# First attention of a four-layer block: loads and weight splits inside it, units begun half a chain apart

## What is computed

```
a = attention(n, n, n, Wq, Wk, Wv, causal) + n          # n = layer norm of x
h = layer_norm(a, gamma, beta)
c = attention(h, context, context, Wcq, Wck, Wcv) + h   # not causal
h = layer_norm(c, gamma, beta)
out = relu(layer_norm(relu(h @ W1 + b1) + h, gamma, beta))
x = x + tanh(g_xattn[0]) * out
```

## Time and profile before

| | us |
|---|---|
| median of 3 runs | 3161.24 (3153.39 to 3162.49) |
| the profiled execution | 3154.09 |
| its span, first to last instruction | 3151.9 |
| start of the first projection (QT of unit 0) | 43.01 |
| start of QT of unit 2 | 160.68 |
| first instruction of the next phase | 293.13 |

### The profile page before, as it was taken

How to read it: one execution, slowest core, us unless ns; L and a number is a source line. 1 busy time by engine, 2 the same in 40 slices (tenths; PEclk the granted TensorE clock), 3 DMA queues, 4 the chain that set the end, 5 groups by cost and what they waited for, 6 DMA issues and landing times. The chain is left out here.

```text
span 3151.9 us, 55831 instructions
## 1 busy us (share of the span) xinstructions
PE 2588.4 (82%) x18079; PEld 2360.7 (75%) x18080; DVE 1555.5 (49%) x3598; ACT 1246.0 (40%) x3047; POOL 1231.6 (39%) x1183
## 2 busy tenths in 40 slices
PE   4674468369979999938997988999689998799992
PEld 4564468269978888828997867888578988789992
DVE  3665545556634444445553324443468777343332
ACT  3232134134543333304553433444357666433330
POOL 0012361564320856041001646640445664266313
PEclk9786689589979999969997889999889999799996
DMA  3041254310010434120000634430611110033312
GB/s 116 1 134 48 72 167 137 94 34 17 16 31 11 140 105 145 33 76 21 15 15 27 222 118 119 114 95 27 191 41 41 55 41 14 28 117 118 109 48 89
DMA packets 139055, 239.80 MB, mean 76 GB/s; under 512 B 17681, under 2 KB 89645, under 8 KB 136609
## 3 DMA queue, kind: packets, MB, share of 16 engines
q1 hardware_dynamic: 65536, 134.62, 13.9%
q10 hardware_dynamic: 59424, 64.09, 6.1%
q0 software_dynamic: 13824, 37.53, 3.9%
HBM read 162.35 MB, written 73.79 MB: 75 GB/s over the span
## 5 line engine op out<-in xcount | busy, mean ns | idle before, releaser
L564 ACT ACTIVATE moe_act<-moe_gu 128x256 f32<-128x256 f32 (+1 forms) x431 | 189.2, 439 | 608.4 <-PE moe_gu L95 608.4
L323 POOL TENSOR_TENSOR moe_wlo<-moe_raw,moe_whi 128x768 fp32r<-128x768 f32 (+1 forms) x170 | 342.1, 2012 | 36.7 <-issue 12.9
L847 DVE TENSOR_TENSOR moe_h<-moe_act,moe_gu 128x256 f32<-128x256 f32 x321 | 134.8, 420 | 367.5 <-ACT moe_act L564 365.5
L352 POOL DMA_INDIRECT moe_whi<-rows_y,moe_slot_r x144 | 139.4, 968 | 423.1 <-DMA rows_y<-moe_y 380.4
L93 PE MATMUL moe_yp<-moe_whi,moe_hThi 128*128 (+1 forms) x926 | 291.2, 314 | 8.9 <-DVE moe_hTlo L863 8.6
L93 PE MATMUL moe_gu<-moe_whi,moe_xThi 128*128 (+2 forms) x706 | 280.4, 397 | 0.1
L95 PE MATMUL moe_gu<-moe_whi,moe_xTlo 128*128 (+2 forms) x706 | 264.3, 374 | 0.0
L94 PE MATMUL moe_gu<-moe_wlo,moe_xThi 128*128 (+2 forms) x706 | 263.9, 374 | 0.0
L94 PE MATMUL moe_yp<-moe_wlo,moe_hThi 128*128 (+1 forms) x926 | 261.0, 282 | 0.0
L95 PE MATMUL moe_yp<-moe_whi,moe_hTlo 128*128 (+1 forms) x926 | 260.4, 281 | 0.0
L863 DVE TENSOR_TENSOR moe_hTlo<-moe_tp,moe_hThi 128x256 fp32r<-128x256 f32 (+1 forms) x275 | 145.1, 528 | 232.1 <-ACT moe_hThi L570 231.1
(11 more groups left out here) (484 smaller groups left out, 7920.8 us busy)
## 6 DMA issues: line engine op xcount, KB each, us to landing
moe_raw<-in_moe_w SPq DMA_DIRECT2D x118, 384.0 KB, 3.2
moe_raw<-in_moe_w SPq DMA_DIRECT2D x52, 512.0 KB, 4.1
moe_xr<-rows_x ACTq DMA_DIRECT2D x69, 256.0 KB, 2.8
rows_y<-moe_y ACTq DMA_DIRECT2D x69, 256.0 KB, 2.2
rows_x<-att_zeros SPq DMA_DIRECT2D x16, 512.0 KB, 6.3
kd<-moe_wlo ACTq DMA_DIRECT2D x32, 256.0 KB, 3.6
vd<-moe_wlo ACTq DMA_DIRECT2D x32, 256.0 KB, 4.0
w_wk_hi<-kd SPq DMA_DIRECT2D x8, 1024.0 KB, 4.8
```

What stands on the lines that cost most here:

```text
L323: pool.tensor_tensor(lo_, cols, hi_.bitcast(F32), ALU.subtract).then_inc(w_done, 1)
L352: pool.indirect_dma_start(out=gath[t % NGA][:, k, :], out_offset=None, in_=rows_y[0:ROWS, :], in_offset=bass.IndirectOffsetOnAxis(ap=slot_ ...
L564: act.activation(act_sb[i % 2][:, :], gu[i % 2][:, 0:HC], func).then_inc(act_done, 1)
```

## The change

The setup block, the split block and the row block go; what they did is inside the attention's block. SP's loads come in the order x of unit 0, three weights, context of unit 0, x of unit 1, four weights, context of unit 1, the rest of x, three constants. The weights lie whole in h2 and in parts of h until they are split; the splits (whole matrices of 128x512) stand in ScalarE's and VectorE's lists ahead of the evictions of nT, QT and KT of unit 0. Eight small loads are issued by ScalarE. GpSimd takes the memsets and the cast of "before", ahead of its first power. Each user waits for just its own load.

`when` has `k * NP / NU` in place of `k // 2 * NP`: unit k begins 8.5 places after unit k - 1. NU stays 2 and NT 4, so sizes and the number of products are the same. In the list, nT of unit 1 follows A of unit 0, n of unit 1 stands between cKT and pT of unit 0, n of unit 2 between cKT and pT of unit 1 (and ahead of h2T of unit 0), and the tail of unit 0 between QT and KT of unit 2, ahead of hT of unit 1. SP stores a unit's context, then loads that of the unit after next.

```
-    when = lambda k, name: k // 2 * NP + {...}
+    PER_UNIT = NT // TB
+    when = lambda k, name: k * NP / NU + {...}
...
-        load_split(nc, name + "w", jobs, D)
...
+        w_raw = [*h2_sb, *h_sb[1:]] if NU == 4 else [y[:, 2 * h:2 * h + 2, :] for y in (*h2_sb, *h_sb) for h in range(2)]
...
+        X_PARTS = [(0, 1), (1, NU), (NU, NK)]
+        SPLITS = {"nT": ("Wq", "Wk"), "QT": ("Wv", "Wck"), "KT": ("Wcv", "Wcq", "W1")}
+        SPLIT_ORDER = [w for ws in SPLITS.values() for w in ws]
...
# SP
+                load_x(0)
+                for name in SPLIT_ORDER[0:3]:
+                    load_w(name)
+                load_c(0)
+                load_x(1)
+                for name in SPLIT_ORDER[3:]:
+                    load_w(name)
+                for k in range(1, NU):
+                    load_c(k)
+                load_x(2)
+                for name in ("below_e", "iota_e", "iota_b"):
+                    sp.dma_start(G[name].ap(), I[name]).then_inc(consts_in, 16)
+                for k in range(NK):
+                    store_c(sp, k)
+                    if k + NU < NK:
+                        load_c(k + NU)
...
# TensorE
+                    if k == 0 and name in USES:
+                        pe.wait_ge(w_lo, SPLIT_ORDER.index(USES[name]) + 1)
...
# ScalarE
+                act.dma_start(ident[:, :], I["ident"]).then_inc(ident_in, 16)
+                for q, name in enumerate(("g_xattn", "g_ffn")):
+                    row(g8[:, 4 * q:4 * q + 4], I[name], 4, gates_in)
+                act.dma_start(causal[:, :, :], I["causal"]).then_inc(mask_in, 16)
+                for dst, src in zip((gamma, beta, b1), rows):
+                    row(dst[:, :], src, D, rows_in)
+                act.dma_start(before[:, :], I["before"]).then_inc(before_in, 16)
+                act.wait_ge(gates_in, 32)
+                act.activation(G["tanh_g"][:, :], g8[:, :], ACT.Tanh).then_inc(gate_set, 1)
+                act.wait_ge(ident_in, 16)
+                act.activation(G["identr"][:, :], ident[:, :], ACT.Copy)
                 for _, k, name in ORDER:
-                    u, i = k % 2, k // 2
+                    u, i = k % NU, k // NU
...
+                    if k == 0 and name in SPLITS:
+                        for w in SPLITS[name]:
+                            act.wait_ge(w_in[W[w]], 16)
+                            act.activation(w_all[0][:, W[w], :, :], w_raw[W[w]][:, :, :], ACT.Copy).then_inc(w_hi, 1)
...
# VectorE
+                    if k == 0 and name in SPLITS:
+                        for w in SPLITS[name]:
+                            v.wait_ge(w_hi, SPLIT_ORDER.index(w) + 1)
+                            v.tensor_tensor(w_all[1][:, W[w], :, :], w_raw[W[w]][:, :, :], w_all[0][:, W[w], :, :].bitcast(F32), ALU.subtract).then_inc(w_lo, 1)
                     if name == "n":
                         s = st_n[u]
+                        for g, (lo, _) in enumerate(X_PARTS):
+                            if k == lo:
+                                v.wait_ge(x_in[g], 16)
...
# GpSimd
+                pool.memset(minus_half[:, :], -0.5)
+                pool.memset(zeros[:, :, :], 0.0)
+                pool.memset(G["ones_bf"][:, :], 1.0)
+                pool.drain().then_inc(zeros_set, 1)
+                pool.wait_ge(before_in, 16)
+                pool.tensor_copy(G["before_bf"][:, :], before[:, :])
...
-        setup_phase(nc, G, I)
```

More of the change, by code:

```diff
@@ L960, in constants @@
     }
[L963 to L991, removed]
 def globals_of(nc, A):
@@ L2176, in single_phase @@
         w_all = hl("w", [P, len(W), KC, D])
[L2177 to L2180, removed]
-        load_split(nc, name + "w", jobs, D)
         U = range(NU)
         per = lambda n, shape: [sb(f"{n}{u}", shape) for u in U]
-        hl_u = lambda n: [hl(f"{n}{u}", [P, 2, 512]) for u in U]
+        hl_u = lambda n: [hl(f"{n}{u}", [P, 2, C]) for u in U]
         n_sb, p_sb, a_sb, h_sb, s_m = (per(n, [P, NT, D]) for n in ("n", "p", "a", "h", "s_m"))
@@ L2197, in single_phase @@
             per_sem(n) for n in ("var_ready", "rstd_ready", "product", "hi_done", "used", "n_stats", "n_ready", "rows_ready", "m_ready", "e_ready", "c_in", "c_out", "gated", "unit_done"))
[L2198 removed]
+        zeroed, zeros_set, rows_in, ident_in, gates_in, consts_in, before_in, mask_in = (
+            sem(n) for n in ("zeroed", "zeros_set", "rows_in", "ident_in", "gates_in", "consts_in", "before_in", "mask_in"))
+        x_in, w_in, w_hi, w_lo, gate_set = [sem(f"x_in{g}") for g in range(3)], [sem(f"w_in{q}") for q in range(len(W))], sem("w_hi"), sem("w_lo"), sem("gate_set")
+        w_raw = [*h2_sb, *h_sb[1:]] if NU == 4 else [y[:, 2 * h:2 * h + 2, :] for y in (*h2_sb, *h_sb) for h in range(2)]
+        before = sb("before", [P, P])
+        g8 = sb("g8", [P, 8])
+        X_PARTS = [(0, 1), (1, NU), (NU, NK)]
+        SPLITS = {"nT": ("Wq", "Wk"), "QT": ("Wv", "Wck"), "KT": ("Wcv", "Wcq", "W1")}
+        SPLIT_ORDER = [w for ws in SPLITS.values() for w in ws]
         minus_half = sb("minus_half", [P, NT])
@@ L2209, in x_of, with store_c @@
             return x[:, k * NT:(k + 1) * NT, :]
+        def store_c(sp, k):
+            sp.wait_ge(used[k % NU], k // NU * NP + at("cT") + 1)
+            for b in range(PER_UNIT):
+                for h in range(2):
+                    sp.dma_start(G["ctxT"][h][PER_UNIT * k + b], cT[k % NU][h][:, :, b * S:(b + 1) * S].bitcast(F32)).then_inc(c_out[k % NU], 16)
         with nc.Block() as block:
@@ L2213, in _ @@
             def _(sp):
[L2214 to L2222, removed]
-        def store_c(sp, k):
-            sp.wait_ge(used[k % 2], k // 2 * NP + at("cT") + 1)
-            for b in range(2):
-                for h in range(2):
-                    sp.dma_start(G["ctxT"][h][2 * k + b], cT[k % 2][h][:, :, b * S:(b + 1) * S].bitcast(F32)).then_inc(c_out[k % 2], 16)
@@ L2230, in single_phase, with load_x @@
-        with nc.Block() as block:
-            @block.sync
-            def _(sp):
-                for k in range(T // NT):
-                    u = k % 2
-                    if k >= 2:
-                        sp.wait_ge(product[u], (k // 2 - 1) * NP + at("cT") + 1)
-                    sp.dma_start(c_raw[u][:, :, :], I["ctx_1024"][2 * k:2 * k + 2].rearrange("b (t p) d -> p (b t) d", p=P)).then_inc(c_in[u], 16)
-                    if k >= 1:
-                        store_c(sp, k - 1)
-                store_c(sp, T // NT - 1)
+                def load_x(g):
+                    lo, hi = (NT * k for k in X_PARTS[g])
+                    sp.dma_start(x[:, lo:hi, :], I["x"][lo // TB:hi // TB].rearrange("b (t p) d -> p (b t) d", p=P)).then_inc(x_in[g], 16)
@@ new lines, in load_w, with load_c @@
+                def load_w(name):
+                    sp.dma_start(w_raw[W[name]][:, :, :], weights[name].rearrange("(k p) d -> p k d", p=P)).then_inc(w_in[W[name]], 16)
+                def load_c(k):
+                    u = k % NU
+                    if k >= NU:
+                        sp.wait_ge(product[u], (k // NU - 1) * NP + at("cT") + 1)
+                    sp.dma_start(c_raw[u][:, :, :], I["ctx_1024"][PER_UNIT * k:PER_UNIT * (k + 1)].rearrange("b (t p) d -> p (b t) d", p=P)).then_inc(c_in[u], 16)
```

36 lines of the change are left out of this document (24 added, 12 removed).

## The result

The changed kernel takes 3190.24 us (median of four, 3181.94 to 3221.53); the kernel before, run beside it, 3157.42 (3153.39 to 3162.49). The profiled execution took 3182.3 with a span of 3180.4, against 3154.09 and 3151.9: 28.5 us more in the span.

What follows compares the result with a forecast made beforehand. No engine was full; in-order evictions and TensorE's clock set the pace. Head 16.2, lead 44.0, strides 59.5 and 68.3, last unit 122.4 sum to 310.4 us against 292.2, +18: 3179 median, range 3155 to 3190.

Steps and rivals of the forecast that it cites:

- the head's landing of "before": First attention's head: constant lands at 8.5 us, so QT of unit 0 starts at 16.2 instead of 43.0, gaining 26.8.
- The third rival: Head: competing loads delay QT of unit 0 to 20.7 or up to 25 us; total 3183 to 3188, chance 0.09.
- The order's waits: TensorE's pauses before A, h2T, F, QT and cQT in the new order: 9.0, 4.6, 7.1, 4.8 and 6.2 us.
- Lead, strides and last unit: First attention from QT of unit 0 to the end: 44.0, 59.5 and 68.3, and 122.4 us, clock included.
- the layout: First attention's steps laid out in queue order; for the old order it gave 290.6 us against 292.2 traced.
- The clock: TensorE's idle stretches lower its granted clock: 34 us lost in the new order instead of 17.
- Cover: Hidden work: SP's zero fill of rows_x ends 70 us before the stage; ScalarE's DMA issue ends before n is wanted.
- Second rival: First attention: the half-chain offset fills VectorE, strides fall below 54 us, 3140 us; chance 0.13 together with a steady clock.
- From the profiled execution to the median: Whole kernel: phases behind the stage unchanged, 7 us added to 3172 profiled, giving a median of 3179.

Runs made afterwards that it cites:

- e3_power: Changed kernel with the cast of "before" moved from ahead of GpSimd's first power to the end of its list; 3186.83 us, ratio 1.0119.
- e2_old_head: Kernel before with only the order changed to half-chain offsets, old head kept; 3197.36 us, ratio 1.0122.
- e4_n_tail: Changed kernel with n at -1.25 instead of -2.5 places and the tail at 18.75 instead of 18.5; 3171.8 us, ratio 1.0052.
- e8_filled_end: Changed kernel with matmuls without use ahead of seven products of unit 3; next phase at 311.2 us, median 3209.24 us.
- e7_best: Changed kernel with eight units, four in flight, the cast at the end of GpSimd's list, n at -0.6, tail at 19.4; 3118.11 us, ratio 0.9878.
- e5_pairs_power: Changed kernel with the old pair order and the cast of "before" behind GpSimd's list; 3153.18 us, ratio 0.9989.

## Why the prediction was wrong, and where it was right

- **The step that failed is the head's landing of "before".** The prediction had the wait (the power, nb, n and nT behind "before") and mis-sized the term. It was set at 8.5 us with bounds 5 and 10.9, from a row in which one queue moved 2 MB; the sum counted the quarter of x ahead of it and not the other 2.8 MB issued before it. It landed at 13.8, outside both bounds, and QT of unit 0 started at 22.04 instead of 16.2: 5.8 us, of which 5.3 are the landing and the rest the cast, which the sum left out, and what follows. e3_power takes the wait away, ends the stage at 309.4, and its median, 3186.83, lies in the range. The third rival had the mechanism (loads that compete) and the time of the first QT, 20.7 to 25, but a chance of 0.09; it had x late as well, which was there at 4.8, named the weights for the upper part, which did not matter, and its total, 3183 to 3188, still ends 2 us short. The Trainium skill (Trainium Kernel Development and Optimization, "Key Constraints") says that the queues share sixteen engines; the 2.56 MB that SP's queue moved before 64 KB of ScalarE's had landed agree, and the sum should have used it.
- **The order's waits**: 8.6, 4.6, 5.5, 4.7 and 5.8 us against 9.0, 4.6, 7.1, 4.8 and 6.2. Lead, strides and last unit came within 1.0 us each, 1.6 in sum; the layout was said to be 1.6 short if it erred as on the old order. The mechanism is right, shown by e2_old_head (+44.1) and e4_n_tail. That the strides fit so closely is in part luck: their waits were forecast 1.8 and 2.6 us too long, and TensorE's own time in them, 43.6 and 46.2, is 2.8 and 2.7 longer than the sum has it (36.3 of products and 4.5 and 7.2 for the clock).
- **The clock**: 17 us more than before was forecast; TensorE's busy time is some 17 us longer for the same products, and e8_filled_end gets 7 of them back. Right in the price: the last four products of unit 3 (cQT, cS, cA and F) took 9.3 us more than their terms at 2.4 GHz, forecast four times 2.3. The granted clock was forecast near 0.6 over the last 60 us and is 0.61; over 43 to 292 us it is 0.81 where 0.76 was forecast, hardly under the 0.82 of the kernel before over the same stretch. So the mean was a poor sign to name: what differs is the time that TensorE works at the lower level, 73.7 us against 41.0, after sixteen falls against eight between the first QT and the end.
- **Cover**: the zero fill of rows_x was issued from 222.8 to 244.1, its last store landed at 249.3, and it ended 68 us before the stage, near the 70 that were said. The splits of 128x512, sized at 0.6 and 0.7 us between nothing and 1.2, took 0.57 and 0.64. Eight DMA issues on ScalarE ran from 0.72 to 5.33 us, 4.6 where at most some 4 were thought, and ended before n was wanted. In the sum on VectorE, twelve low parts of 1.2 us are 14.4, not 14.0; the 44 us stand.
- **Second rival**: refuted for this order (60.4 and 68.4, not below 54); e7_best, with an offset and four units in flight, fills VectorE to 80%.
- **From the profiled execution to the median**: 7 us were added as a constant, and the phases behind were carried over unchanged. On the profiled execution the forecast was 3172 and 3182.3 was measured: 5.8 of the head, 1.6 of the layout, 2.9 behind the stage, where the sum had nothing. The step to the median came out at 7.9, near the 7, but by luck: half the executions are long, and the two long ones that were profiled are so by the third attention. Three sets of the changed kernel have medians of 3190.2, 3193.0 and 3194.7, all above the range, which had no term for it.

## What to carry to other kernels

Price a load by the bytes that are ahead of it on all queues, not by its own size or its own queue: here 64 KB landed when 3.3 MB had moved. That is a price and no order, since two loads issued ahead of it on the other queue landed behind it. Let nothing urgent stand in an engine's list behind a constant that is wanted only later; e3_power got 8 us by this, e5_pairs_power nothing, because there another wait ended last. When independent chains share in-order engines, what stands ahead of an eviction that the matmul engine waits for matters as much as how far apart they start: moving two short steps, by 1.25 places and a quarter, gave back 26 of the 44 us that the offset cost. After such a change, look for a stretch in which one chain is left alone, since its pauses bring the granted clock down as well (0.61 over the last 60 us here).

## What was not expected of the hardware

- The same 64 KB load took 9.3 us as the eighth on ScalarE's queue and 3.5 close behind the first load on SP's. As the eighth on ScalarE's it still landed ahead of 768 KB issued before it on SP's.
- The granted clock fell to 0.50 in the third attention while TensorE was busy 40.00 of 40.00 us. With such falls that phase took some 32 us longer in two profiled executions of one kernel than in a third.
- Matmuls without use, put ahead of a lonely chain's products, made that chain 7 us shorter.
